# Attention of a transformer layer on one Trainium2 core: the order of scores, key tiles and transpose within a step

## What is computed

```python
q = (hidden_states @ Wq).reshape(b, s, NUM_HEADS, HEAD_DIM)
k, v = (kv[..., :HEAD_DIM], kv[..., HEAD_DIM:])
scores = jnp.einsum('bqhd,bkd->bhqk', q, k) * scale
scores = jnp.where(causal[None, None], scores + bias[None], -jnp.inf)   # ALiBi bias
attn = jax.nn.softmax(scores, axis=-1)
out = jnp.einsum('bhqk,bkd->bqhd', attn, v).reshape(b, s, h)
```

## Time and profile before

| | before |
|---|---|
| median of 3 runs | 813.38 us |
| the profiled execution's own time | 815.24 us |
| span of its trace | 813.5 us |
| TensorE busy | 802.1 us (99%) |
| VectorE busy | 596.2 us (73%) |
| GpSimd busy | 427.7 us (53%) |
| ScalarE busy | 370.5 us (46%) |

### The profile page before, as it was taken

The page is one execution under the profiler, slowest core; times in us unless marked ns, Lnnn a source line. Parts: engine busy times, 40 slices in busy tenths (PEclk is TensorE's granted clock), DMA queues, the critical chain, the costliest instruction groups (busy, mean ns, idle before and its releaser), DMA issues.

```text
span 813.5 us, 13624 instructions
## 1 busy us (share of the span) xinstructions
PE 802.1 (99%) x4608; PEld 582.3 (72%) x4608; DVE 596.2 (73%) x1592; ACT 370.5 (46%) x728; POOL 427.7 (53%) x311
## 2 busy tenths in 40 slices
PE   7999999999999999999999999999999999999997
PEld 5788888888656555656565555688887888888886
DVE  5885575657878889988888997364647779684878
ACT  2757355312466777676666665221401141041322
POOL 1000000000389988899898888522746288363465
PEclk9999999999999999999999999999999999999999
DMA  9867666566556555665556645452064523500112
GB/s 344 309 216 250 226 242 231 174 191 195 159 133 147 134 144 144 153 160 134 133 159 168 166 108 178 153 176 90 1 226 146 171 79 111 191 35 1 39 66 104
DMA packets 71389, 125.84 MB, mean 155 GB/s; under 512 B 7460, under 2 KB 16708, under 8 KB 71240
## 3 DMA queue, kind: packets, MB, share of 16 engines
q1 hardware_dynamic: 70592, 123.66, 49.6%
q10 hardware_dynamic: 728, 1.32, 0.5%
HBM read 85.61 MB, written 38.94 MB: 153 GB/s over the span
## 4 chain that ended last, share of the span: by engine, by line
PE 91%; DMA 4%; POOL 2%; DVE 1%; issue 1%; ACT 1%; ACTq 0%; SPq 0%; DVEq 0%; POOLq 0%
PE p_s L869 12%; PE p_st L898 10%; PE p_o L909 10%; PE p_o L808 7%; PE p_s L808 6%; PE p_o L922 5%; PE p_s L977 5%; PE p_s L979 5%; PE p_s L978 5%; PE p_o L810 4%; PE p_s L810 3%; PE p_s L1001 3%; PE p_s L1002 3%; PE p_st L1002 2%; PE p_st L1001 2%; PE p_st L977 2%
## 5 line engine op out<-in xcount | busy, mean ns | idle before, releaser
L1462 DVE CUSTOM_DVE_ANT_0 spill<-p_s,mask 128x128 bf16<-128x128 f32 (+3 forms) x512 | 219.5, 483 | 41.2 <-PE p_s L869 40.9
L1168 ACT ACTIVATE pt<-p_st 128x512 f32<-128x512 f32 (+1 forms) x352 | 178.1, 562 | 101.8 <-PE p_st L898 101.6
L637 POOL TENSOR_SCALAR_AFFINE_SELECT pt<-pt 128x512 f32<-128x512 f32 x128 | 88.0, 700 | 234.7 <-ACT pt L1168 234.7
L869 PE MATMUL p_s<-kst,xt 98*128 98x128 f32 (+3 forms) x512 | 151.3, 343 | 0.9 <-DVE mx L1462 0.7
L898 PE MATMUL p_st<-xt,kst 100*128 100x512 f32 (+1 forms) x352 | 129.7, 388 | 0.3 <-ACT pt L1168 0.2
L869 PEld LDWEIGHTS p_s<-kst,xt 98*128 98x128 f32 x512 | 91.7, 189 | 52.9 <-DVE mx L1462 42.5
L644 POOL TENSOR_TENSOR pt<-pt 128x1536 f32<-128x1536 f32 x32 | 112.3, 3508 | 2.7
L909 PE MATMUL p_o<-pt,vst 128*32 128x512 f32 (+3 forms) x1024 | 83.1, 442 | 0.0
L650 POOL TENSOR_TENSOR pt<-pt 128x1024 f32<-128x1024 f32 x32 | 76.7, 2396 | 0.0
L898 PEld LDWEIGHTS p_st<-xt,kst 100*128 100x128 f32 x352 | 64.7, 191 | 13.6 <-issue 5.6
L808 PE MATMUL p_o<-xt,wqh 128*128 128x512 f32 x136 | 53.1, 400 | 0.8 <-DVE xt L1618 0.8
(11 more groups left out here) (206 smaller groups left out, 1619.4 us busy)
## 6 DMA issues: line engine op xcount, KB each, us to landing
xt<-qh_d SPq DMA_DIRECT2D x64, 256.0 KB
qh_d<-qh SPq DMA_DIRECT2D x32, 256.0 KB, 2.1
ql_d<-ql SPq DMA_DIRECT2D x32, 256.0 KB, 2.2
xt<-ql_d SPq DMA_DIRECT2D x32, 256.0 KB
o_d<-o_st SPq DMA_DIRECT2D x32, 256.0 KB, 2.1
ob<-o_d SPq DMA_DIRECT2D x32, 256.0 KB, 4.6
xs<-in_x_t_dram SPq DMA_DIRECT2D x28, 256.0 KB, 5.4
xin<-in_x_dram SPq DMA_DIRECT2D x14, 512.0 KB, 5.9
```

Source lines behind the costliest of these rows:

```text
L637: pool.affine_select(out=own, in_=own, compare_op=ALU.is_ge, fill=0.0, base=0, pattern=[[0, 4], [1, P]], channel_multiplier=-1).then_inc(c ...
L869: pe.matmul(scores_of(n), qst[s % 4][0:R_MAX, j, qb * P:(qb + 1) * P], kst[0:R_MAX, b * S:b * S + keys], start=True, stop=True).then_inc(s ...
L1168: act.activation(pt[s % 2][:, j:j + heads, PT_AT[kb]:PT_AT[kb] + KB_LEN[kb]], p_st[:, place(k) % 3, 0:heads * KB_LEN[kb]].rearrange("p (j ...
L1462: dve.tensor_tensor_reduce(spill[:, SPILL_AT[qb]:SPILL_AT[qb] + keys], scores_of(n), mask[:, S - keys:S], 1.0, LOWEST, ALU.add, ALU.max, m ...
```

## The change

A head's scores are now dealt in three pieces: `A` is block 1 and then block 0 (256 columns, then 128), `B` block 2, `C` block 3, each counted for itself over the heads. The string puts three of the four `A` directly in front of a group, moves `T` behind the fourth tile (u3), and deals `B` and `C` unevenly. `TURN_AT` goes from 2 to 4, so the transposed maxima take the ring's place behind u3. VectorE takes the maxima in the order `TAKEN`, and the waits on both sides count by the two tables. Its other work stays at the same i, but for `max_low`, which goes from i = 3 to i = 4.

```diff
--- before.py
+++ after.py
@@ -51,7 +51,7 @@
 UNITS = tuple((kb, j, 1) for kb in (0, 1) for j in range(4)) + ((2, 0, 2), (2, 2, 2), (3, 0, 4))
 NU = len(UNITS)
 
-TURN_AT = 2
+TURN_AT = 4
 RING = NU + 1
 
 UNITS_TO = (4, 8, 10, 11)
@@ -274,6 +274,10 @@
         BANK, BANK_AT = (0, 0, 1, 2), (0, P, 0, 0)
         BANK_LAST = (1, 1, 2, 3)
 
+
+        TAKEN = (0, 1, 2, 3, 6, 4, 5, 7, 10, 11, 8, 9, 12, 13, 14, 15)
+        WRITTEN = (1, 0, 2, 3, 6, 5, 4, 7, 10, 11, 9, 8, 13, 12, 14, 15)
+
         def xt(b, low):
             return (xt0 if b % 2 == 0 else xt1)[:, CK * low:CK * low + CK, :]
 
@@ -294,6 +298,14 @@
         def qw_loads(e):
             return sum(i % 4 != 1 for i in range(e + 1))
 
+        def taken(n):
+
+            return n + 1 if n < 32 else 16 * (n // 16) + TAKEN.index(n % 16) + 1
+
+        def written(n):
+
+            return n + 1 if n < 32 else 16 * (n // 16) + WRITTEN.index(n % 16) + 1
+
         def scores_of(n):
             qb = n % 4
             return p_s[:, BANK[qb], BANK_AT[qb]:BANK_AT[qb] + (qb + 1) * P]
@@ -306,7 +318,7 @@
             return (p_st[:, 1, :] if b == 0 else p_mean)[0:2 * TPB, 0:P]
 
         def turned_max(s):
-            return p_st[:, (TURN_AT if s > 0 else 2) % 3, 0:P]
+            return p_st[:, (TURN_AT if s > 1 else 2) % 3, 0:P]
 
         def wo_half(w, h):
             return ob[:, h % 4, :] if w is ob else w[:, h // 2, S * (h % 2):S * (h % 2) + S]
@@ -861,17 +873,20 @@
                     pe.wait_ge(q_freed, CK * LASTB + 1)
                     pe.wait_ge(kst_ext, B)
                     pe.wait_ge(k_done, 2)
-                if n % 16 == 0:
+                if written(n) % 16 == 1:
                     pe.wait_ge(q_in[s % 4], 64 * (s // 4) + 64)
-                if qb != 1:
-                    at_least(pe, max_done, n - qb - 4 + BANK_LAST[qb] + 1)
+
+                if n >= 4 and qb != (1 if n < 32 else 0):
+                    pe.wait_ge(max_done, taken(n - qb - 4 + BANK_LAST[qb]))
                 keys = (qb + 1) * P
                 pe.matmul(scores_of(n), qst[s % 4][0:R_MAX, j, qb * P:(qb + 1) * P],
                           kst[0:R_MAX, b * S:b * S + keys], start=True, stop=True).then_inc(s_done, 1)
 
             def free_bank(s, at):
                 before = RING * s + at - 3
-                if before % RING == TURN_AT:
+                if (s, at) == (0, 2):
+                    pe.wait_ge(ml_done, 2)
+                elif before % RING == TURN_AT:
                     at_least(pe, ml_done, min(before // RING + 2, STEPS))
                 elif before >= 0:
                     k = before % RING
@@ -927,7 +942,9 @@
 
 
 
-            ORDER = "xuxuxTGxuxuxuxuGuxuxxuuxGxu"
+
+            ORDER = "uuAGBuCuTBuuAGCuBuCuuAGAuBC"
+            BLOCKS = {"A": (1, 0), "B": (2,), "C": (3,)}
 
             GROUP = (((0,), ()), ((1, 2, 3), ()), ((), (0, 1)))
 
@@ -935,17 +952,18 @@
 
             def attend(s):
                 n, units, groups = 4 * (4 * s + AHEAD), 0, 0
+                heads = {"A": 0, "B": 0, "C": 0}
                 for what in ORDER:
                     if what == "u":
                         score_t(s, units)
                         units += 1
                         if (s, units) in FIRST_AT:
                             first_tiles(FIRST_AT[s, units])
-                    elif what == "x":
-                        for _ in range(2 if n % 4 == 0 else 1):
+                    elif what in BLOCKS:
+                        for qb in BLOCKS[what]:
                             if n < 4 * HEADS_ALL:
-                                score(n)
-                            n += 1
+                                score(n + 4 * heads[what] + qb)
+                        heads[what] += 1
                     elif what == "T":
                         if 0 < s < STEPS - 1:
                             turn_max(s + 1)
@@ -1455,9 +1473,10 @@
                     dve.wait_ge(mx_clear, 2)
                 if n % 16 == 0:
                     at_least(dve, mt_done, s - 1)
-                at_least(dve, max_done, n - 3)
+                if n >= 4:
+                    dve.wait_ge(max_done, taken(n - 4))
                 if qb != 1:
-                    dve.wait_ge(s_done, n + 2 if qb == 0 else n + 1)
+                    dve.wait_ge(s_done, max(written(n), written(n + 1)) if qb == 0 else written(n))
                 keys = (qb + 1) * P
                 dve.tensor_tensor_reduce(spill[:, SPILL_AT[qb]:SPILL_AT[qb] + keys], scores_of(n),
                                          mask[:, S - keys:S], 1.0, LOWEST, ALU.add, ALU.max,
@@ -1481,13 +1500,13 @@
             def attend(s):
                 first = 4 * (4 * s + AHEAD)
                 for i in range(16):
-                    if first + i < 4 * HEADS_ALL:
-                        maximum(first + i)
+                    if first < 4 * HEADS_ALL:
+                        maximum(first + TAKEN[i])
                     if s == 0 and i == 11:
                         q_low(CK * B - 1)
                     if s == STEPS - 2 and i == 0:
                         o_normal(5)
-                    if i == 3 and 0 < s < STEPS - 1:
+                    if i == 4 and 0 < s < STEPS - 1:
                         max_low(s + 1)
                     if i % 4 == 1 and s > GROUPS and s % GROUPS in (2, 3, 4, 5):
                         invert(s // GROUPS - 1, 4 * (s % GROUPS - 2) + i // 4)
```

## The result

The change makes the kernel much slower: 992.38 us (992.11 to 992.50, 4 runs) against 813.29 us, a ratio of **1.220** (95% interval 1.218 to 1.221), where 859.6 was forecast. The profiled execution has a span of 990.7 us, 177.2 more than before. Every instruction is still there; the time is in the 32 steps of attention.

The account below looks back on a forecast made before the run. TensorE's sequence of starts was taken as the path. 29 x (0.50 + 0.60 - 0.20) = 26.1, plus 9.6, 7.6 and 2.9 for the third wait, make 46.2; 813.4 + 46.2 = 859.6 us, 8-in-10 range 842 to 871.

Parts of the forecast that it names:

- TensorE's own step: TensorE's step without new waits: pairs in front of groups, T's move and the old waits' end save 0.20 us, to 9.19.
- Wait 1: Tile u3 to u5: u5 waits for ScalarE's exponential of u3 to free its ring place, 0.50 us per step.
- wait 2: Block 3 of head 1 to block 3 of head 2, behind G1: wait for the bank through VectorE, 0.60 us per step.
- Wait 3: Head 3's pair behind the totals waits for VectorE's other work and maxima: 0.60 us in 16 steps, 0.76 in 10.
- Rival C: Waits make TensorE's clock fall in the attention: 10 to 20 us more, 870 to 880 us; chance 0.09.
- No gain given back: GpSimd, DMA and the end stage get slack but give no time back, since the end stage starts from the last step.
- step 0 at +0.8: In step 0, which has no groups, wait 1 and wait 2 stand less masked: 0.8 us more.
- T, a cost of 0.02: T behind u3, between tiles, holds TensorE 0.11 us, a cost of about 0.02 per step; its later result is hidden.
- a rule on the distance of matmuls: Matmul distance as columns / 2.4 + 2.5 ns: the order's gain would be about 0.09 instead of 0.20, the time 862.8 us.

Follow-up runs that it names:

- second new order: Another string with all the change's means, other work behind i = 0: 837.71 us; with output work one step later and step 0's low part at i = 3: 807.19 us.
- experiment 6: Two kernels from the kernel before: only T moved behind the fourth tile, 820.39 us; only the short pairs turned to 256 then 128 columns, 812.47 us.
- Experiment 7: The kernel of experiment 2 with the second block-3 score behind G1 moved behind the last two tiles before the totals' pair: 842.05 us.
- Experiments 1 to 4: experiment 1, experiment 2, experiment 3, and a fourth: the kernel before with VectorE's other work behind i = 13 instead of i = 9, 927.85 us.
- experiment 2: The changed kernel with VectorE's other work at full size behind i = 6 instead of i = 9: 845.12 us.
- experiment 3: The changed kernel with each of GpSimd's two additions per step cut into four pieces, one per head: 864.07 us.
- experiment 5: The changed kernel with three more rounds of zero-weight totals matmuls in the gap behind the totals, in 26 steps: 931.02 us.
- experiment 1: The changed kernel with VectorE's other work in the attention cut from 512 to 8 columns: 971.13 us.

## Why the prediction was wrong

The direction and the three places were right; the time is outside the range. By its own steps:

- **TensorE's own step, gain 0.20 to 9.19.** Right, as far as it can be seen. The second new order has all means of the change without their waits, and its steps are 9.17 to 9.20; it is another string, so it bears out the size of the gain and not each term. That a 128-column score in front of a group saves something was nowhere in the trace and was bounded between rows; in after the pair holds 0.27 there where 0.28 was taken (405.46 to 405.73 in its timeline). The terms were not all measured alone: turning the pairs round gave 1.5 us (experiment 6), one pair in front of a group with the block-3 scores further apart another 1.5.
- **Wait 1 (0.50) and wait 2 (0.60).** Right. The steps without other work are 10.26 where 10.3 was forecast (s = 2). The distances are 1.10 and 1.40, a little under the 1.14 and 1.46 that the prediction called the least possible. Experiment 7 moved wait 2 alone, and it shrank.
- **Wait 3: the step that failed.** The chain "0.59, 0.62, then 0.94 for the low part of the output weights, ..." was the right chain, with one wrong term. 0.94 was the mean of that operation at its old place, and the change moved it into GpSimd's addition, where it takes 3.43 to 3.70. With 3.43 the prediction's sum gives 2.85 + 2.49 - 2.23 = 3.1 us; measured are 3.3. Over 26 steps this is 86 us instead of 20. The terms that it added to wait 3 for the normalised output (0.16) and for an inversion (0.26) don't show: the end of the addition decides, and the wait is the same in all 26 steps. The prediction named the neighbour once, in the upper end of its range ("VectorE's longer records next to GpSimd"), at 0.3 us per step; it cost 2.5 to 2.8 on top of the 0.94. Experiments 1 to 4 show the cause: the length of GpSimd's instruction sets the duration, not the operation's own size, it goes when the operation stands elsewhere, and the old order suffers the same.
- **Rival C, the clock.** It had a chance of 0.09 and a price of 10 to 20 us; it came beside the forecast, not instead of it, and cost 60.5. Its premise was wrong too: waits 1 and 2 leave the clock at 1.00 (experiment 2), and so does a wait 3 of 0.85 us (experiment 3). The rule that the prediction cites there from the Trainium skill, page "TensorE: Matmul & The Clock Gate" (section A second HAM failure mode: psum-queue depth-cycling), of frequent small gaps that make the clock swing, is not borne out by these two. The clock fell behind gaps of 3.3 us, and of 2.75 in experiment 1. The price per fall was taken from a stretch of 5 us with a mean of 0.77, which gave 1.15; the 26 falls that experiment 5 took away cost 60.5, 2.3 us each.
- **No gain given back, step 0 at +0.8.** Step 0 was mispriced in the same way: its low part of Q, at i = 11, met the addition. In after it takes 1.92 us and the first values start 1.4 us later. In the kernel of experiment 2 the first values start 1.6 us later than in before, and step 1 is 11.62 instead of 10.09.
- **T, a cost of 0.02.** The steps of 9.18 have T behind u3 too, which fits it. In the old order the move costs 0.2, as a wait for the ring (experiment 6). The last two steps, costed at nothing, are 1.3 us longer.
- Slips without consequence: what the rows and the prediction call step 20 is, by its low part of an output, step 21. And the 0.8 us by which the 29 present steps exceed 29 x 9.39 lie mostly in step 1 (10.09), where the clock falls, and not only at the change of a sequence.

Of the 177.2 us between the two spans: 86.4 block, 60.5 clock, and 30.3 that remain with experiment 2, of which 299.4 - 273.1 = 26.3 lie in the 29 steps, 1.6 ahead of them and 1.3 in the last two steps; 1.1 lie behind the start of the last values and were not traced.

The page "SBUF — State Buffer" of the Trainium skill has the missing rule (section Who interferes with whom): GpSimd shares a pair of SBUF ports with VectorE, the pair is an exclusive lock for a whole instruction, the one that issues first has it, and VectorE needs it for an operation with two SBUF inputs when GpSimd reads SBUF, not for one with a single one. The traces agree: 2.91 us for eight columns beside an addition, 0.35 for the inversion beside the same. The prediction weighed a rule on the distance of matmuls, worth 3 us, and not this one. The page "TensorE: Matmul & The Clock Gate" of the Trainium skill (section HAM oscillation — how this bites in real kernels) reckons the loss as the throttled time multiplied by a half. For the 162.2 - 11.5 us that experiment 5 took away this makes 75 us, an estimate by that page; measured are 60.5. Part of the slow stretches lies inside waits, as that from 444.8, which begins 0.95 us before wait 3 of its step ends (445.75); whether this makes up the whole difference was not measured. The rule on distances that the prediction took from the same page of the Trainium skill (section Back-to-back issue gap) is there the gap of an isolated matmul. The section adds that it counts too little at few columns in a stream with weight loads, and the 0.23 us of the earlier trace rows against its 0.165 agrees.

## What to carry to other kernels

An operation that moves keeps its work, not its duration: take its duration from what stands beside it at the new place, above all for a VectorE operation with two inputs in SBUF and a GpSimd instruction of 3.5 us. A mean that lies above the shortest record of the same form (0.94 against the 0.69 of the earlier trace rows) is a hint that a neighbour is in it; here all 16 records behind that mean end 0.55 us after an instruction of GpSimd. When an order is rewritten by hand, lay the other engines' timelines beside it; the same reordering ideas gave 992 us with the other work in the wrong place and 807 with it in the right one.

## What the runs showed of the hardware

- A VectorE operation with two SBUF inputs ends 0.55 us (512 columns) or 0.02 us (8 columns) after the GpSimd addition that was under way at its start, in all 26 steps with other work of after and of experiment 1. GpSimd's mask with one input blocks it too: 0.99 beside a mask of 0.63.
- It goes the other way round as well. In before the low part of Q starts at 217.01, 0.05 ahead of the first addition, and that addition takes 3.97 instead of 3.49:

```profile
217.06 3.97 POOL L644 TENSOR_TENSOR pt<-pt 128x1536 f32<-128x1536 f32 x1
```

- More matmuls can make a kernel faster: zero-weight work in a gap of 3.3 us kept TensorE's granted clock at 1.00 (2.4 GHz) and gave back 61 us of 992.
